# Cross-attention scores of a decoder layer: stacks of 64 rows in both halves of the partitions in place of one of 72

## The reference, cut to what matters

```
q = (Q @ Wq + bq).reshape(b, -1, H, HD)      # H = 16, HD = 8, 256 tokens in each of 2 batches
k = (K @ Wk + bk).reshape(b, -1, H, HD)      # 512 context tokens
scores = einsum('bhqd,bhkd->bhqk', q, k) / sqrt(HD)
scores = where(mask == 0, -inf, scores)
attn = softmax(scores, axis=-1)
ctx = einsum('bhqk,bhkd->bhqd', attn, v)
```

## Time and profile before

| | |
|---|---|
| median of 3 runs (lowest, highest) | 204.1 us (203.88, 204.63) |
| the profiled execution's own time | 204.96 us |
| its span, first to last instruction | 203.1 us |
| busy: PE, PEld, DVE, ACT, POOL | 192.5, 152.6, 156.9, 137.1, 96.6 us |
| mean granted TensorE clock | 0.992 |
| `k_stack` loads | 18 of 128 KB |
| `q_stack` loads | 6 of 144 KB, 6 of 48 KB |

### The profile page before, as it was taken

One profiled execution on the slowest core, in us unless ns is written; L12 is line 12 of the kernel. 1 busy time (PEld: TensorE's weight loads), 2 busy tenths in 40 slices (PEclk: granted clock), 3 DMA queues, 4 the chain that ended last, 5 costly groups with the idle time before them and its releaser, 6 DMA issues.

```text
span 203.1 us, 4608 instructions
## 1 busy us (share of the span) xinstructions
PE 192.5 (95%) x1626; PEld 152.6 (75%) x1626; DVE 156.9 (77%) x414; ACT 137.1 (67%) x318; POOL 96.6 (48%) x145
## 2 busy tenths in 40 slices
PE   7899999899999899996999999999799999999995
PEld 7778877677877676765666757656468799999994
DVE  2569998668768895979889999998963876458744
ACT  2399968688668687676889989989687232452220
POOL 7579307778476678607729993000420017500430
PEclk9999999999999999998899999999999999999999
DMA  6980406803555015589502400000000000000001
GB/s 161 380 222 4 155 2 194 276 0 47 64 60 65 5 40 125 83 121 128 132 0 61 98 2 0 5 0 3 0 3 0 5 0 0 3 0 13 3 1 38
DMA packets 13301, 12.69 MB, mean 62 GB/s; under 512 B 1072, under 2 KB 11312, under 8 KB 13280
## 3 DMA queue, kind: packets, MB, share of 16 engines
q1 hardware_dynamic: 12176, 11.15, 25.4%
q10 hardware_dynamic: 1008, 1.06, 1.6%
q0 software_dynamic: 96, 0.20, 0.6%
HBM read 10.96 MB, written 1.44 MB: 61 GB/s over the span
## 4 chain that ended last, share of the span: by engine, by line
PE 76%; DVE 10%; issue 4%; DMA 3%; ACT 2%; POOL 2%; SPq 1%; DVEq 0%
PE ps L994 13%; PE ps L953 12%; PE ps L1018 8%; PE ps L879 7%; PE ps L930 7%; PE ps L895 6%; PE ps L912 6%; PE ps L763 6%; PE ps L851 4%; DMA wk<-in_L_xattn_Wk 3%; PE ps L776 3%; DVE low L1218 3%; DVE q_t L1228 2%; ACT prob L636 2%; DVE prob_t L1291 1%
## 5 line engine op out<-in xcount | busy, mean ns | idle before, releaser
L1228 DVE CUSTOM_DVE_ANT_0 q_t<-ps,mask_add 128x512 f32<-128x512 f32 x64 | 41.4, 685 | 2.5 <-PE ps L912 2.5
L510 POOL TENSOR_TENSOR prob<-prob,rec 128x512 f32<-128x512 f32 x32 | 32.7, 1048 | 21.9 <-DVE rec L1287 21.9
L636 ACT ACTIVATE prob<-ps,low 128x256 f32<-128x256 f32 x64 | 29.5, 485 | 7.0 <-DVE low L1218 7.0
L670 ACT ACTIVATE q_t<-q_t,low 128x512 f32<-128x512 f32 x44 | 29.4, 723 | 0.0
L953 PEld LDWEIGHTS ps<-ident,q_t 128*128 128x128 f32 x176 | 20.5, 146 | 5.9 <-issue 3.5
L1218 DVE TENSOR_REDUCE low<-ps 128x2 f32<-128x512 f32 x32 | 20.5, 684 | 5.9 <-PE ps L851 5.8
L656 ACT ACTIVATE q_t<-ps 128x512 f32<-128x512 f32 x18 | 10.6, 599 | 21.1 <-PE ps L994 21.1
L549 POOL TENSOR_TENSOR place_k<-place_k 128x256 f32<-128x256 f32 x10 | 7.3, 735 | 36.3 <-DVE place_k L1253 36.3
L953 PE MATMUL ps<-ident,q_t 128*128 128x128 f32 x176 | 24.3, 283 | 0.3 <-DVE prob L1345 0.3
L1274 DVE TENSOR_TENSOR q_t<-q_t,ps 128x512 f32<-128x512 f32 x18 | 12.2, 685 | 11.3 <-PE ps L994 7.0
L912 PE MATMUL ps<-k_stack,q_stack 72*128 72x512 bf16 x64 | 19.4, 390 | 0.0
(11 more groups left out here) (184 smaller groups left out, 470.3 us busy)
## 6 DMA issues: line engine op xcount, KB each, us to landing
k_stack<-k_dram SPq DMA_DIRECT2D x18, 128.0 KB
wg<-in_L_ffn_w_gate SPq DMA_DIRECT2D x1, 1024.0 KB, 5.5
wu<-in_L_ffn_w_up SPq DMA_DIRECT2D x1, 1024.0 KB, 8.0
q_stack<-q_dram SPq DMA_DIRECT2D x6, 144.0 KB
k_dram<-prob SPq DMA_DIRECT2D x1, 768.0 KB, 3.6
w_in<-in_L_attn_Wq ACTq DMA_DIRECT2D x2, 256.0 KB, 5.8
context<-in_ctx SPq DMA_DIRECT2D x1, 512.0 KB, 6.2
w_in<-in_L_attn_Wv SPq DMA_DIRECT2D x1, 512.0 KB, 8.1
```

The source lines that it names most:

```text
L510: nc.gpsimd.tensor_tensor(pr, pr, rec1[:, s % 2, r, :].unsqueeze(2).to_broadcast([P, C, S]), ALU.mult).then_inc(s_norm1, 1)
L636: e = nc.scalar.activation(prob1[:, s % 3, r, c * S:(c + 1) * S], ps[:, 2 * (s % 2) + r, c * S:(c + 1) * S], ACT.Exp, bias=low1[:, s % 2, ...
L670: nc.scalar.activation(prob2[n % 3][:, c, :], score2[n % 2][:, c, :], ACT.Exp, bias=low2[:, n % 2, c:c + 1], scale=-1.0).then_inc(s_exp2, 1)
L1228: nc.vector.tensor_tensor_reduce(out=score2[n % 2][:, c, :], in0=ps[:, 2 * (n % 2) + c, :], in1=mask_add[:, c, :], scale=1.0, scalar=3e38, ...
```

## The change

The lowest pair of parts (third part of the keys with third part of the queries) is left out, which leaves eight pairs, 64 rows (`KROWS`): three pairs for key parts 0 and 1, and two for key part 2 (`PRODUCTS` = (3, 3, 2)). The keys' 64 rows are loaded twice, to partitions 0 to 63 and to partitions 64 to 127. The queries of chunk 0 go to partitions 0 to 63, those of chunk 1 to partitions 64 to 127, each with 128 tokens of a batch. The two matmuls of a head then use one half of the partitions each; their columns and their PSUM banks stay as they were. The key DMAs of a batch become 16 instead of nine, of the same shape and size. The query DMAs of a batch become 12 instead of six, each with 128 tokens (256 bytes) a row and head instead of 256 tokens (512 bytes); those of key part 2 have 16 rows.

```
-KSTACK = PARTS * PARTS * HD2
+PRODUCTS = tuple(PARTS - (j == PARTS - 1) for j in range(PARTS))
+KROWS = sum(PRODUCTS) * HD2
...
-        k2_stack = sb("k2_stack", [KSTACK, B, H2, SK], BF16)
+        k2_stack = sb("k2_stack", [C * KROWS, B, H2, SK], BF16)
...
-        q2_stack = sb("q2_stack", [KSTACK, H2, T], BF16)
+        q2_stack = sb("q2_stack", [C * KROWS, H2, T], BF16)
...
                 for j in range(PARTS):
-                    for i in range(PARTS):
-                        r = (j * PARTS + i) * HD2
-                        load(k2_stack[r:r + HD2, b, :, :],
-                             k2_dram[j, :, b * SK:(b + 1) * SK].rearrange("(d h) t -> d h t", d=HD2), d_kstack[b])
+                    for i in range(PRODUCTS[j]):
+                        for c in range(C):
+                            r = c * KROWS + (j * PARTS + i) * HD2
+                            load(k2_stack[r:r + HD2, b, :, :],
+                                 k2_dram[j, :, b * SK:(b + 1) * SK].rearrange("(d h) t -> d h t", d=HD2), d_kstack[b])
...
                 for i, (first, last) in enumerate(QSETS):
-                    for j in range(PARTS):
-                        r = j * PARTS * HD2
-                        load(q2_stack[r:r + PARTS * HD2, first:last, b * S:(b + 1) * S],
-                             rows[:, first:last, :], d_qstack[b][i])
+                    for c in range(C):
+                        for j in range(PARTS):
+                            r, count = c * KROWS + j * PARTS * HD2, PRODUCTS[j] * HD2
+                            load(q2_stack[r:r + count, first:last, b * P:(b + 1) * P],
+                                 rows[0:count, first:last, c * P:(c + 1) * P], d_qstack[b][i])
...
                 if h == 0:
-                    pe.wait_ge(d_kstack[b], 16 * PARTS * PARTS)
+                    pe.wait_ge(d_kstack[b], 16 * C * sum(PRODUCTS))
                 for i, (first, _) in enumerate(QSETS):
                     if h == first:
-                        pe.wait_ge(d_qstack[b][i], 16 * PARTS)
+                        pe.wait_ge(d_qstack[b][i], 16 * C * PARTS)
...
-                    t = b * S + c * P
-                    mm(ps[:, 2 * (n % 2) + c, :], q2_stack[:, h, t:t + P],
-                       k2_stack[:, b, h, :], start=True, stop=True).then_inc(s_score2, 1)
+                    rows = slice(c * KROWS, (c + 1) * KROWS)
+                    mm(ps[:, 2 * (n % 2) + c, :], q2_stack[rows, h, b * P:(b + 1) * P],
+                       k2_stack[rows, b, h, :], start=True, stop=True).then_inc(s_score2, 1)
```

## The result

The changed kernel takes 222.45 us in the median of four executions (219.89 to 224.26), against 203.99 for the kernel before on the same chip; the ratio is 1.083 (1.078 to 1.087). So it is about 17 us slower, where 14 were forecast. The ratio is that of the two undisturbed executions (219.89 and 221.69 us); the profiled execution (224.26 us) is one of the two disturbed ones and the slowest of the four.

What follows compares the result with a forecast made beforehand. DVE, with 1.3 us of slack, capped TensorE's gain; the key loads' pace on SP's queue would make queries late. 13.8 (second wait) + 1.5 (clock) - 1.2 (pairs) = +14.1 us, so 218 us; 8-in-10 range 207 to 225.

Steps and rivals of the forecast that it cites:

- part 2: Key loads of batch 0: 16 at 2.07 us each, ending at 81.1 us instead of 66.6.
- Rival (a): Key loads overlap in part, 1.4 to 1.6 us each; only batch 1 late: 204 to 209 us, chance 0.10.
- part 3: Queries of batch 0 land at 86.5 us behind the keys; TensorE stands still 5.8 us before head 0.
- the DMA that the prediction named as the sign: At both TensorE waits, the profile was to show a DMA of `q_stack` or `k_stack` as releaser.
- part 4: Batch 1: queries queue behind keys and `wd`, reaching head 16 at 127.5 us; shift of 13.8 us replaces the earlier 5.8.
- part 5: After the second wait: low clock costs 1.5 us, faster pairs give back 1.2; feed-forward untouched.
- part 1: Cross-attention score matmuls side by side: 0.23 instead of 0.44 us a pair, 3 us gain at most.
- DVE's idle time: Sign for the cross-attention between the two waits: DVE's idle time near nothing.
- Rival (b): Key loads under about 1.4 us stay hidden, leaving the pairs' gain: 201.6 us, chance 0.11.

Runs made afterwards that it cites:

- e5: Changed kernel with stacked key rows first laid out in DRAM by 32 copies, read back in 16 loads of 8 rows a batch: 217.76 us, ratio 1.073.
- e6: Changed kernel with stacked key rows laid out in DRAM by copies, read back in 8 loads of 16 rows a batch: 204.54 us, ratio 1.0038.
- e3: Changed kernel with the load of wd issued after the queries of batch 1 instead of ahead of them: 214.34 us, ratio 1.040.
- e9: Changed kernel with unread identity matmuls filling TensorE's waits, 26 ahead of head 0 and 46 ahead of head 16: 219.33 us, ratio 1.079.
- e4: Changed kernel with 50 unread identity matmuls ahead of head 0 and 95 ahead of head 16, sized too long: 235.33 us, ratio 1.153.
- e1: Kernel before with only the lowest product left out: 64 rows, no twin, 8 key loads a batch: 206.47 us, ratio 1.014.
- e7: Changed kernel with stacked key rows laid out in DRAM by copies, read back in one load of 128 rows a batch: 204.70 us, ratio 1.0050.
- e8: Kernel before with its 18 key loads replaced by DRAM copies and one load of 72 rows a batch: 203.26 us, ratio 0.9992.
- e10: e7 with every cross-attention score matmul over all 128 rows, output wrong but work the same in size: 204.85 us, ratio 1.0066.

## Why the prediction was right, and where it was off

The forecast was +14.1 us. By the ratio the kernel rose by 0.083 x 204 = 16.9 us; the span of the profiled execution rose by 222.4 - 203.1 = 19.3. The steps below are read from the profile, so they have to add up to 19.3.

- **The pace of an 8-row load (part 2): right.** 0.58 of the DMA engines and 63 GB/s, against 0.58 and 66 before the change; SP went on at 82.84 us, forecast 82.3. e5 and e6 show the mechanism. Rival (a), overlap of the twins, is refused by the same 63 GB/s. That the forecast was met within 0.6 us is partly luck: with identical loads SP went on at 83.83 us in e3, 81.66 in e9 and 80.52 in e4.
- **The first wait (part 3): right.** TensorE started at 86.65 us against a forecast of 86.5. The releaser in the trace is "issue" and not the DMA that the prediction named as the sign.
- **The second wait (part 4): right in its steps, 4 us short.** 131.59 us against 127.5. Two terms were too small in this execution. The keys of batch 1 moved at 68 GB/s (92 to 104 us), 1.95 us a load and not 1.78: SP came free of `wd` at 122.5, not 119.2. And from there to the end of the store it was 5.4 us (122.54 to 127.92), where the forecast had 4.1 (119.2 to 123.3, of them 3 for `wd`'s tail). The first of the two varies between executions: in e9, with the same loads, SP was free at 117.07 and done with the store at 122.44, 0.9 us ahead of the forecast. e3 confirms that `wd` is in this path.
- **The clock (part 5): 1.7 us, forecast 1.5.** Shown by e9. The low clock at TensorE's restart was expected from the earlier trace rows.
- **The gain of the pairs (part 1): wrong, and the one step whose mechanism failed.** "A pair of 512 columns will cost 0.23 instead of 0.44 us" was read from pairs in the middle of twelve such pairs. In the cross-attention nearly every pair has full-height transposes behind it and about half of the pairs have them ahead; the pair costs 0.31 us, and the transposes take back 0.06 to 0.15. 0.2 us a head becomes next to nothing (e1, e7, e8, e10). Nor did DVE's idle time fall: between the waits it was 0.60 of 13.60 us (the row below), in the earlier trace rows 1.26 of 31.10.
- **Rival (b), a faster kernel with hidden loads.** e6 and e7 are that case, with hidden key loads, and they are 0.4 and 0.5% slower than before. Its gain of 2 to 3 us rested on the price of the pair, of which 0.2 us was left behind head 16.

```profile
99.40:113.00 13.60, 12.17 (x103) 8.19 (x104) 13.00 (x35) 11.60 (x22) 9.09 (x17) 1.00 0.80 89
```

From head 16 to the end the kernel before took 203.1 - 113.70 = 89.4 us and the changed one 90.8. That is 1.4 us more, where the forecast had 0.3 (1.5 for the clock less 1.2 for the pairs). With the 4.1 us of part 4 this makes the 5.2 us by which the profiled execution was over the forecast. By the ratio the time was 3 us over the forecast. How those 3 us split isn't shown, since only the one execution left a trace.
What stays open: what e7 would take without its wait of 1.49 us at head 16, since a version with hidden keys and only six query loads was not run; why a change between 64 rows and full height costs time; why the keys of batch 1 moved faster than those of batch 0 before the change (1.78 us a load against 2.07) and hardly faster after it; and why identical loads vary by 10% or more between profiles (63 and 71 GB/s). Issuing part of the loads on another engine's queue was not tried.

## What to carry to other kernels

When a change multiplies small loads, price them by the measured time of one such load and add them on their queue, in order, up to the instruction that needs the last one; here nine loads were through some 7 us before the next store, and 16 were not. Look at the DMA share while they run: at 0.5 to 0.6, as here, more rows in a load took the delay away (e6); another queue was not tried. And read the price of a narrow matmul from its neighbours' starts too: a pair that runs side by side showed its full saving only where several stood in a row.

## What the runs showed of the hardware

- Matmuls of 64 rows among transposes of full height cost TensorE time at the change: eight transposes with a pair on either side took 1.03 us instead of 0.87 or 0.88 (e1, e7 against the kernel before and e8). Behind value products of 128 x 32 nothing was added (0.32 and 0.33 us). Stacks of 72 and of 128 rows cost the same (0.44 and 0.45 us a pair, e8 and e10).
- With the same bytes, loads of 16 and 128 partitions moved 140 and 416 GB/s in packets of about 16 KB. Loads of 8 partitions moved 99 to 119 GB/s in such packets in one batch and 70 in the other (e5), and 63 to 77 in packets of 1 KB.
- SP itself is held up in issuing: 16 loads of 8 rows in packets of 1 KB took 18.26 us to issue where nine had taken 6.37, and the load behind them 15.65 us. The same 16 loads in packets of about 16 KB took 5.79 us (e5), but the load behind the next 16 took 23.13.
- Behind its wait of 11.75 us TensorE worked at a granted clock of 0.52 (131.6 to 135.4 us); kept busy through the wait, it stayed at 1.00 (e9), which was worth 1.7 us.
